# A transformer block on one core: the normalised input transposed by TensorE, or loaded a second time with features on partitions

## The chip, the core and the metric

The kernel runs on one core of a Trainium2 chip. Five engines share the work, each with its own queue of instructions that it executes in order: TensorE (PE) multiplies, VectorE (DVE) and ScalarE (ACT) read its results from PSUM and compute on them, GpSimd (POOL) computes beside them, and the sync engine (SP) issues nearly all DMAs. Engines wait for each other at semaphores. The metric is the device time of one launch in microseconds (us), as the median of several runs.

## The reference

The input x has 4 sequences of 2048 positions with 512 features in float32. The block is a linear-attention layer and a low-rank feed-forward layer, each behind a layer norm and with a residual:

```python
x = x + attn(layernorm(x))            # attn normalises once more: x_norm = layernorm(.) * ln_g + ln_b
# in attn, with z = layernorm(x):
qkv  = x_norm @ W_qkv + b_qkv
gate = sigmoid(z @ W_gate + b_gate); gate = gate / (mean(gate) + EPS)
q, k = relu(q * gate)**2 + EPS, relu(k * gate)**2 + EPS     # 16 heads of 32
kv_s += k_t (x) v_t;  k_s += k_t;  out_t = (q_t . kv_s) / (q_t . k_s + EPS)   # over positions t
return out @ W_proj + b_proj
x = x + gelu(layernorm(x) @ U1 @ V1 + b1) @ U2 @ V2 + b2    # ranks 128, 2048 hidden
```

Two norms in a row come down to a mean and two row factors. With the mean mu and the variance var of a row of x, z = (x - mu) * r with r = (var + EPS)^-1/2, and the second norm multiplies z by (r*r*var + EPS)^-1/2.

## The kernel before

The 64 chunks of 128 positions are taken in turn: step (p, b) starts chunk 4p + b, which is row block p of sequence b. Within a step, one chunk n is projected to gate, key, query and value, the chunk before it (c) goes through scores, state and output projection, the one before that (d) is normalised again and enters the feed-forward layer, which works on groups of two chunks over two steps. So steps differ by the parity of b: an odd step also computes the group's first product with U1 and the last product of an earlier group. Every float32 operand of the large products is split into a high and a low part (float32r tiles named _hi and _lo) and three products are accumulated.

All orders are written out by hand, engine by engine, in the function `step` of each engine. The path of the input that the change touches is:

- SP loads a chunk into `xs`, positions on partitions (`load_x`, L250), three steps ahead.
- DVE takes its mean and variance (`x_stats` L516, `x_moments` L522), at the end of the step two ahead; POOL makes the row factors from them in six operations on one column (`small_stats`, helper L328).
- DVE writes `zs` = (x - mu) * r (`x_norm`, L531), behind the query's evacuation in the step before the chunk's own.
- PE transposes `zs` in four 128x128 blocks into the bank `ps_t` (`tz`, helper `transpose4` L772), behind the output product L964 and ahead of the feed-forward products `h_pair` and `q_pair`. A transpose of the same helper is made of the queries, the keys and the second norm's rows.
- ACT copies the bank to `zt_hi` (`z_head`, L419), DVE subtracts it from the bank into `zt_lo` (`z_tail`, L547). These two are the stationary operands of the four projections (`project`).
- DVE evacuates the gate (L616) and key, query and value (L581, L653), the latter three multiplied by the second row factor.
- POOL adds the output bias to `xs` (`add_bias`, L355), once `zs` is taken, and makes the low parts of the hidden layer and of the keys (`h_tail` L366, L392) around it.

Names in the rows: `ps_q` and `ps_h` are banks of the feed-forward layer, `h_hi` and `h_lo` the parts of its hidden tile, `ot_hi` and `ot_lo` those of the attention output; L979 and L980 are the running sums over the keys, which reuse the bank `ps_b` of that output, and so wait for `ot_lo` (DVE L679). `carry_rows` is a row in DRAM through which the key sums of a sequence go from one row block to the next, stored by L293 and read back to all partitions by L300.

Of the kernel before, what the change touches and what calls it, by code (L numbers as in the profile page):

```python
# [29 lines left out]
P = 128  # L30
# [73 lines left out]
def block_kernel(nc, x, ln_g, ln_b, w_qkv, b_qkv, w_gate, b_gate, w_proj, b_proj,  # L104
                 u1, v1, b1, u2, v2, b2, out, carry_dram):
    ctx = ExitStack()
    with ctx:
# [34 lines left out]
        xs = sb("xs", [P, 4, DM])  # L142
        x1s = sb("x1s", [P, 4, DM])
# [9 lines left out]
        stats, moments = sb("stats", [P, 4, 6]), sb("moments", [P, 4, 2])  # L153
        small = sb("small", [P, 4, 6])
# [22 lines left out]
        def bank(name):  # L177
# [13 lines left out]
            x_stats x_small z_ready xb_ready tz_done zt_hi_ready zt_ready  # L191
# [9 lines left out]
        x_in = [sem(f"x_in{i}") for i in range(4)]  # L201
        stored = [sem(f"stored{i}") for i in range(4)]
# [41 lines left out]
        def _(sp):  # L244
            def load_x(c):
                if not c.exists:
                    return

                wait(sp, s["x1_steps"], Chunk(c.p, c.off - 4).done(3, 1))
                sp.dma_start(xs[:, c.slot, :], x[c.slot, bass.ds(c.row, P), :]).then_inc(x_in[c.slot], 16)  # L250

# [23 lines left out]
            load_tiles(range(8))  # L275
# [5 lines left out]
            def step(p, b):  # L281
                if isinstance(p, int) and 4 * p + b < 2:
                    load_tiles((range(FIRST + 6, FIRST + 9), range(FIRST + 9, len(tiles)))[b])
# [26 lines left out]
        def _(pool):  # L310
# [19 lines left out]
            def small_stats(c):  # L330
# [4 lines left out]
                var, r, done = moments[:, c.slot, 1:2], small[:, c.slot, :], s["x_small"]  # L335
# [4 lines left out]
                pool.wait_ge(done, c.done(6, 1))  # L340
                tiny(r[:, 1:2], r[:, 0:1], minus_half[:, :], ALU.pow, done)
                pool.wait_ge(done, c.done(6, 2))
                tiny(r[:, 2:3], r[:, 1:2], r[:, 1:2], ALU.mult, done)
                pool.wait_ge(done, c.done(6, 3))
                tiny(r[:, 3:4], r[:, 2:3], var, ALU.mult, done)
                pool.wait_ge(done, c.done(6, 4))
                tiny(r[:, 5:6], r[:, 3:4], eps_col[:, :], ALU.add, done)
                pool.wait_ge(done, c.done(6, 5))
                tiny(r[:, 4:5], r[:, 5:6], minus_half[:, :], ALU.pow, done)

            def add_bias(c):

                if c.exists:
                    pool.wait_ge(s["z_ready"], c.done())
# [4 lines left out]
            small_stats(Chunk(0, 0))  # L359
            small_stats(Chunk(0, 1))  # L360
# [8 lines left out]
            def step(p, b):  # L369
# [3 lines left out]
                if d.exists:  # L373
# [3 lines left out]
                        .then_inc(s["x1b_ready"], 1)  # L377
                if ffn.exists and b % 2 == 0 and not is_last(p):
                    h_tail(ffn, pairs[0])
                if n.exists:  # L380
# [3 lines left out]
                        .then_inc(s["key_ready"], 1)  # L384
                if ffn.exists and not is_last(p):
# [3 lines left out]
                add_bias(Chunk(p, b + 1))  # L389
# [19 lines left out]
        def _(act):  # L409
# [6 lines left out]
            def z_head(c):  # L416
                if c.exists:
                    act.wait_ge(s["tz_done"], c.done())
                    E.activation(zt_hi[:, :, :].rearrange(flat), ps_t[:, :], ACT.Copy)\  # L419
                        .then_inc(s["zt_hi_ready"], 1)  # L420
# [9 lines left out]
            tile_heads(range(KT))  # L430
            z_head(Chunk(0, 0))
            tile_heads(range(KT, 6))
# [4 lines left out]
            tile_heads(range(6, FIRST))  # L437
# [67 lines left out]
        def _(dve):  # L505
            E = nc.vector

            def x_stats_wait(c):

                if c.exists:  # L510
                    dve.wait_ge(x_in[c.slot], c.dmas())
                    wait(dve, s["x_small"], Chunk(c.p, c.off - 4).done(6, 6))
# [5 lines left out]
            def x_moments(c):  # L518


                if c.exists:
                    E.bn_aggr(moments[:, c.slot, :], stats[:, c.slot, :]).then_inc(s["x_stats"], 1)  # L522

            def x_norm(c):

                if c.exists:
                    dve.wait_ge(s["x_small"], c.done(6, 2))
                    before = Chunk(c.p, c.off - 3)
                    if before.exists:
# [12 lines left out]
            x_norm(Chunk(0, 0))  # L542
# [21 lines left out]
            tile_tails(range(KT))  # L564
            z_tail(Chunk(0, 0))
            tile_tails(range(KT, 10))
# [34 lines left out]
            def step(p, b):  # L601
# [12 lines left out]
                if n.exists:  # L614
                    dve.wait_ge(s["gate_done"], n.done())
                    E.tensor_tensor(gate[:, :], ps_b[:, :], bias[:, GATE, :], ALU.add)\  # L616
# [8 lines left out]
                    dve.wait_ge(s["x_small"], n.done(6, 6))  # L625
# [18 lines left out]
                x_norm(Chunk(p, b + 1))  # L644
# [92 lines left out]
                if c.exists:  # L737

                    dve.wait_ge(s["x1_small"], c.done(2, 2))
                    after = Chunk(p, b + 1)  # L740
                    if after.exists:
                        dve.wait_ge(s["tz_done"], after.done())
                    elif d.exists:
# [14 lines left out]
        def _(pe):  # L758
# [34 lines left out]
            def tz(c):  # L793
                if not c.exists:
                    return
                pe.wait_ge(s["z_ready"], c.done())
                before = Chunk(c.p, c.off - 2)
                if before.exists:
# [31 lines left out]
            def step(p, b):  # L830
# [16 lines left out]
                if c.exists:  # L847
                    pe.wait_ge(s["den_steps"], c.done(6, 6))

                    if n.exists:  # L850
                        pe.wait_ge(s["zt_ready"], n.done())
# [170 lines left out]
```

## Time and profile before

| | |
|---|---|
| median of 3 runs | 1840.01 us (1838.84 to 1841.26) |
| profiled execution | 1837.18 us |
| its span in the trace | 1835.1 us |
| granted TensorE clock, mean | 0.996 |
| PE busy | 1792.8 us, 98% |
| DVE busy | 1449.0 us, 79% |
| POOL busy | 799.2 us, 44% |
| ACT busy | 683.7 us, 37% |
| DMA | 61.06 MB, 33 GB/s |

The profiled execution is one launch; the span is what the trace covers of it, and some 2 us lie around it. Busy times are unions of the instructions' spans on an engine. A matmul's span in the trace is its latency, and the next one starts before it ends, so what a matmul takes from TensorE is read from the distance of two starts and not from its duration. The profile's lines name tiles as out<-in and the line of the kernel.

### The profile page before, as it was taken

Reading aid. Unit: us, or ns where it says so; the run is one execution under the profiler, and the core shown is the slowest. Engines: PE = TensorE matmul, PEld = TensorE weight load, DVE = VectorE, ACT = ScalarE, POOL = GpSimd, SP = SyncE. Lnnn points to the kernel's source line nnn. Section 1 sums busy time; section 2 is a strip of 40 time slices with the busy share of each in tenths; the row PEclk is TensorE's granted clock in tenths of the full one; section 3 lists DMA queues with packets and bytes.
Section 4 is the critical chain, followed back from the end, with each engine's and each line's share of the span. In section 5 each row is a group of like instructions: output and inputs, shape, how many; then the busy total and the mean of one; then the engine's idle time right before and its main releaser. Section 6 shows DMA issues by size and latency. Waiting matters only on the chain.

```text
span 1835.1 us, 34352 instructions
## 1 busy us (share of the span) xinstructions
PE 1792.8 (98%) x13753; PEld 1535.6 (84%) x13753; DVE 1449.0 (79%) x2606; ACT 683.7 (37%) x1242; POOL 799.2 (44%) x1027
## 2 busy tenths in 40 slices
PE   6899999999999999999999999999999999999997
PEld 3688888888888888888888888888888888888876
DVE  6877888878788788787788788788788788788775
ACT  4233433333433333433333433433333333333332
POOL 3344445434444434444444444444444444354430
PEclk9999999999999999999999999999999999999999
DMA  6101010011010011010010000010100110100000
GB/s 197 39 18 35 24 36 24 24 35 36 24 36 24 24 36 33 26 35 24 24 35 27 33 27 26 31 35 24 36 24 24 36 35 25 35 24 24 29 19 24
DMA packets 34508, 61.06 MB, mean 33 GB/s; under 512 B 3672, under 2 KB 6256, under 8 KB 34352
## 3 DMA queue, kind: packets, MB, share of 16 engines
q1 hardware_dynamic: 33488, 57.31, 9.8%
q8 instruction: 110, 1.80, 0.4%
q10 hardware_dynamic: 864, 1.57, 0.3%
q14 instruction: 46, 0.38, 0.1%
HBM read 41.96 MB, written 16.91 MB: 32 GB/s over the span
## 4 chain that ended last, share of the span: by engine, by line
PE 92%; DVE 1%; POOL 0%; ACT 0%; issue 0%; DVEq 0%
PE ps_a L767 9%; PE ps_a L766 9%; PE ps_a L765 9%; PE ps_t L772 6%; PE ps_b L767 6%; PE ps_b L766 6%; PE ps_b L765 6%; PE ps_q L765 4%; PE ps_b L964 3%; PE ps_h L765 3%; PE ps_h L766 3%; PE ps_h L767 3%; PE ps_q L766 3%; PE ps_q L767 3%; PE ps_c L942 3%; PE ps_c L954 3%
## 5 line engine op out<-in xcount | busy, mean ns | idle before, releaser
L366 POOL TENSOR_TENSOR h_lo<-h_full,h_hi 128x512 fp32r<-128x512 f32 x244 | 313.6, 1285 | 500.0 <-DVE h_hi L593 500.0
L447 ACT ACTIVATE h_full<-ps_h,cols 128x256 f32<-128x256 f32 x512 | 211.0, 472 | 241.6 <-PE ps_h L767 233.8
L593 DVE CAST h_hi<-h_full 128x512 fp32r<-128x512 f32 x256 | 176.1, 688 | 97.4 <-ACT h_full L447 97.4
L765 PE MATMUL ps_b<-wx_hi,zt_hi 128*128 128x512 f32 x512 | 206.0, 402 | 2.0 <-DVE key_sums L695 1.7
L765 PE MATMUL ps_a<-wx_hi,zt_hi 128*128 128x512 f32 x512 | 207.6, 405 | 0.0
L767 PE MATMUL ps_b<-wx_hi,zt_lo 128*128 128x512 f32 x512 | 202.7, 396 | 0.0
L766 PE MATMUL ps_b<-wx_lo,zt_hi 128*128 128x512 f32 x512 | 202.5, 396 | 0.0
L767 PE MATMUL ps_a<-wx_hi,zt_lo 128*128 128x512 f32 x512 | 202.2, 395 | 0.0
L766 PE MATMUL ps_a<-wx_lo,zt_hi 128*128 128x512 f32 x512 | 201.7, 394 | 0.0
L328 POOL TENSOR_TENSOR small<-moments,eps_col 128x1 f32<-128x1 f32 x128 | 25.7, 201 | 394.1 <-DVE moments L734 325.8
L765 PE MATMUL ps_q<-h_hi,u_hi 128*128 128x256 f32 x512 | 159.3, 311 | 7.1 <-DVE h_lo L598 5.1
L458 ACT ACTIVATE query_t<-ps_t 128x512 f32<-128x512 f32 x64 | 38.2, 597 | 323.3 <-PE ps_t L772 323.3
L765 PE MATMUL ps_h<-pt_hi,v_hi 128*128 128x256 f32 x512 | 152.1, 297 | 0.9 <-DVE pt_lo L647 0.9
L766 PE MATMUL ps_h<-pt_lo,v_hi 128*128 128x256 f32 x512 | 144.8, 283 | 0.0
L767 PE MATMUL ps_h<-pt_hi,v_lo 128*128 128x256 f32 x512 | 143.9, 281 | 0.0
L766 PE MATMUL ps_q<-h_lo,u_hi 128*128 128x256 f32 x512 | 143.7, 281 | 0.0
L767 PE MATMUL ps_q<-h_hi,u_lo 128*128 128x256 f32 x512 | 143.5, 280 | 0.0
L765 PEld LDWEIGHTS ps_q<-h_hi,u_hi 128*128 128x128 f32 x512 | 96.4, 188 | 26.1 <-POOL h_lo L366 13.2
L473 ACT ACTIVATE key_t<-ps_t 128x512 f32<-128x512 f32 x64 | 38.3, 598 | 210.7 <-PE ps_t L772 210.7
L767 PEld LDWEIGHTS ps_b<-wx_hi,zt_lo 128*128 128x128 f32 x512 | 96.2, 188 | 23.3
L765 PEld LDWEIGHTS ps_b<-wx_hi,zt_hi 128*128 128x128 f32 x512 | 96.5, 189 | 22.5 <-DVE zt_lo L547 2.1
L767 PEld LDWEIGHTS ps_a<-wx_hi,zt_lo 128*128 128x128 f32 x512 | 96.0, 187 | 22.8
(159 smaller groups left out, 5047.9 us busy)
## 6 DMA issues: line engine op xcount, KB each, us to landing
xs<-L_attn_x SPq DMA_DIRECT2D x64, 256.0 KB, 2.7
out<-x1s SPq DMA_DIRECT2D x64, 256.0 KB, 2.1
key_sums<-carry_rows SPq DMA_DIRECT2D x60, 256.0 KB, 3.2
x1s<-L_attn_W_qkv SPq DMA_DIRECT2D x8, 256.0 KB, 5.1
x1s<-L_attn_W_gate SPq DMA_DIRECT2D x4, 256.0 KB, 4.1
h_full<-L_attn_W_qkv SPq DMA_DIRECT2D x4, 256.0 KB, 6.1
x1s<-L_ffn_U SPq DMA_DIRECT2D x4, 256.0 KB, 3.4
carry_rows<-key_sums SPq DMA_DIRECT2D x64, 2.0 KB
```

What stands on the lines that cost most here:

```text
L366: E.tensor_tensor(h_lo[:, i % 2, :], h_full[:, i % 2, :], h_hi[:, i % 2, :].bitcast(F32), ALU.subtract).then_inc(s["h_lo_ready"], 1)
L447: last = E.activation(h_full[:, i % 2, a * GROUP:(a + 1) * GROUP], ps_h[i % 2][:, a * GROUP:(a + 1) * GROUP], ACT.Gelu_apprx_tanh, bias=b1 ...
L458: E.activation(query_t[:, :, :].rearrange(flat), ps_t[:, :], ACT.Copy)\
L473: E.activation(key_t[:, :, :].rearrange(flat), ps_t[:, :], ACT.Copy)\
L593: E.tensor_copy(h_hi[:, i % 2, :], h_full[:, i % 2, :]).then_inc(s["h_hi_ready"], 1)
L765: E.matmul(ps, wh, mh, start=start and i == 0, stop=False)
L766: E.matmul(ps, wh, ml, start=False, stop=False)
L767: mm = E.matmul(ps, wl, mh, start=False, stop=stop and i == last)
L772: mm = E.transpose(ps_t[:, k * P:(k + 1) * P], src[:, k * P:(k + 1) * P], ident[:, :])
L942: mm = E.matmul(ps_scores[j][:, ft * P:(ft + 1) * P], key_t[rows, ft, :], query_t[rows, ft, :], start=True, stop=True, tile_position=(HEAD ...
L954: mm = E.matmul(ps_c[:, cols], keys[:, c.half, cols], values[:, c.half, cols], start=True, stop=True)
L964: mm = E.matmul(ps_b[HEAD * j:HEAD * (j + 1), ft * P:(ft + 1) * P], values[:, c.half, h * HEAD:(h + 1) * HEAD], probs[:, j, ft * P:(ft + 1 ...
```

## The change

A second copy of the input, laid out with features on partitions (`x_turned`: for each chunk 128 rows of 512 values, four blocks of 128 positions side by side), is passed to the kernel and loaded into `xt`, two chunks deep. The row means go through DRAM to all partitions: SP stores one column of 128 means into `rows_dram` and reads it back as a row of 128 values on every partition (`turn_rows`). POOL subtracts it from `xt` in place (`center`). ACT and DVE make `zt_hi` and `zt_lo` from `xt` in SBUF. `x_norm`, `tz` and the `zs` of the first norm are gone. What stood in `zs` as the factor r now multiplies the gate's evacuation, and the factor of the other three evacuations becomes (var + EPS * (var + EPS))^-1/2, in five operations on a column. `add_bias` follows `center` and stands earlier in POOL's step.

```diff
 def load_x(c):   # SP
     sp.dma_start(xs[:, c.slot, :], x[c.slot, bass.ds(c.row, P), :]).then_inc(x_in[c.slot], 16)
+    wait(sp, s["zt_ready"], Chunk(c.p, c.off - 2).done())
+    sp.dma_start(xt[:, c.half, :, :].rearrange(flat), x_turned[c.slot, c.row // P, :, :])\
+        .then_inc(xt_in[c.slot], 16)
...
+def turn_rows(c):   # SP, at the start of step for Chunk(p, b + 1)
+    sp.wait_ge(s["x_stats"], c.done(2, 2))
+    sp.dma_start(rows_dram[c.slot, :].rearrange("(t a) -> t a", a=1), small[:, c.slot, 2:3]).then_inc(rows_out[c.slot], 16)
+    sp.wait_ge(rows_out[c.slot], c.dmas())
+    wait(sp, s["z_ready"], Chunk(c.p, c.off - 2).done())
+    sp.dma_start(rows[:, c.half, :],
+                 rows_dram[c.slot, :].rearrange("(a t) -> a t", a=1).broadcast_to([P, P]))\
+        .then_inc(rows_in[c.slot], 16)
...
 load_x(Chunk(0, 0))
-load_tiles(range(8))
+load_tiles(range(6))
+turn_rows(Chunk(0, 0))
+load_tiles(range(6, 8))
...
+def center(c):   # POOL
+    mine = xt[:, c.half, :, :]
+    pool.wait_ge(xt_in[c.slot], c.dmas())
+    pool.wait_ge(rows_in[c.slot], c.dmas())
+    E.tensor_tensor(mine, mine, rows[:, c.half, :].unsqueeze(1).broadcast_to([P, KT, P]),
+                    ALU.subtract).then_inc(s["z_ready"], 1)
 def add_bias(c):
-    pool.wait_ge(s["z_ready"], c.done())
+    pool.wait_ge(s["x_stats"], c.done(2, 1))
...
 def z_head(c):   # ACT
-    act.wait_ge(s["tz_done"], c.done())
-    E.activation(zt_hi[:, :, :].rearrange(flat), ps_t[:, :], ACT.Copy)
+    act.wait_ge(s["z_ready"], c.done())
+    act.wait_ge(s["value_done"], before.done())
+    E.activation(zt_hi[:, :, :].rearrange(flat), xt[:, c.half, :, :].rearrange(flat), ACT.Copy)
...
-def x_norm(c):   # DVE
-    dve.wait_ge(s["x_small"], c.done(6, 2))
-    dve.wait_ge(s["tx_done"], before.done())
-    E.tensor_scalar(zs[:, :], xs[:, c.slot, :], moments[:, c.slot, 0:1], small[:, c.slot, 1:2],
-                    ALU.subtract, ALU.mult).then_inc(s["z_ready"], 1)
 def z_tail(c):
-    E.tensor_tensor(zt_lo[:, :, :].rearrange(flat), ps_t[:, :],
+    E.tensor_tensor(zt_lo[:, :, :].rearrange(flat), xt[:, c.half, :, :].rearrange(flat),
                     zt_hi[:, :, :].rearrange(flat).bitcast(F32), ALU.subtract)
...
-    E.tensor_tensor(gate[:, :], ps_b[:, :], bias[:, GATE, :], ALU.add)
+    E.scalar_tensor_tensor(out=gate[:, :], in0=ps_b[:, :], scalar=small[:, n.slot, 1:2],
+                           in1=bias[:, GATE, :], op0=ALU.mult, op1=ALU.add)
...
-def tz(c):   # PE
-    pe.wait_ge(s["z_ready"], c.done())
-    pe.wait_ge(s["probs_ready"], before.done(HPG, HPG))
-    transpose4(zs, s["tz_done"])
-tz(Chunk(0, 0))
...
-    tz(Chunk(p, b + 1))
     if ffn.exists:
         h_pair(ffn, pairs[3])
         q_pair(ffn, pairs[2])
```

On TensorE, in an even step of the steady state, this stands behind the output product L964 before (names as above, zs being the normalised rows):

```order
L964 MATMUL ps_b<-probs,values 32x128 x16
L772 MATMUL ps_t<-ident,zs 128x128 x4
L765 MATMUL ps_h<-pt_hi,v_hi 128x256
L766 MATMUL ps_h<-pt_lo,v_hi 128x256
L767 MATMUL ps_h<-pt_hi,v_lo 128x256
L765 MATMUL ps_h<-pt_hi,v_hi 128x256
L766 MATMUL ps_h<-pt_lo,v_hi 128x256
L767 MATMUL ps_h<-pt_hi,v_lo 128x256
```

And in the changed kernel, where the same product is L980 and the lines of the three-part product are L793 to L795:

```order
L980 MATMUL ps_b<-probs,values 32x128 x16
L793 MATMUL ps_h<-pt_hi,v_hi 128x256
L794 MATMUL ps_h<-pt_lo,v_hi 128x256
L795 MATMUL ps_h<-pt_hi,v_lo 128x256
L793 MATMUL ps_h<-pt_hi,v_hi 128x256
L794 MATMUL ps_h<-pt_lo,v_hi 128x256
L795 MATMUL ps_h<-pt_hi,v_lo 128x256
L793 MATMUL ps_q<-h_hi,u_hi 128x256
```

The four transposes have gone, and the feed-forward products follow the output product at once.

On POOL, an even step before begins with the feed-forward bias (x1s), and has the attention bias (xs) ahead of the keys' low part:

```order
L376 TENSOR_TENSOR x1s<-x1s,bias_out 128x512
L366 TENSOR_TENSOR h_lo<-h_full,h_hi 128x512
L383 TENSOR_TENSOR keys<-keys,eps_col 128x512
L366 TENSOR_TENSOR h_lo<-h_full,h_hi 128x512
L355 TENSOR_TENSOR xs<-xs,bias_proj 128x512
L392 TENSOR_TENSOR key_lo<-keys,key_hi 128x512
L366 TENSOR_TENSOR h_lo<-h_full,h_hi 128x512 x2
```

In the changed kernel L377 is the centering:

```order
L406 TENSOR_TENSOR x1s<-x1s,bias_out 128x512
L377 TENSOR_TENSOR xt<-xt,rows 128x512
L384 TENSOR_TENSOR xs<-xs,bias_proj 128x512
L396 TENSOR_TENSOR h_lo<-h_full,h_hi 128x512
L416 TENSOR_TENSOR keys<-keys,eps_col 128x512
L396 TENSOR_TENSOR h_lo<-h_full,h_hi 128x512
L427 TENSOR_TENSOR key_lo<-keys,key_hi 128x512
L396 TENSOR_TENSOR h_lo<-h_full,h_hi 128x512 x2
```

The centering and the attention bias now stand between the feed-forward bias and the first low part of the hidden tile.

On SP, the end of an even step and the start of an odd one before, from the second load on (key_sums is the read of the carried sums, out the store of results):

```order
L250 DMA xs<-L_attn_x 128x512
L254 DMA out<-x1s 128x512 x2
L293 DMA carry_rows<-key_sums 1x512
L300 DMA key_sums<-carry_rows 128x512
L250 DMA xs<-L_attn_x 128x512
```

And in the changed kernel, from the load of xs on (L264 and L267 are the two DMAs of `turn_rows`):

```order
L254 DMA xs<-L_attn_x 128x512
L256 DMA xt<-x_turned 128x512
L264 DMA turned_rows<-small 128x1
L267 DMA rows<-turned_rows 128x128
L273 DMA out<-x1s 128x512 x2
L315 DMA carry_rows<-key_sums 1x512
L322 DMA key_sums<-carry_rows 128x512
L254 DMA xs<-L_attn_x 128x512
```

The load of `xt` and the two DMAs of the means now stand ahead of the stores and of the carried sums.

## Rows read from the trace of the kernel before

**Rows 1.** The page: busy time and share of each engine; the chain by engine.
```profile
PE 1792.8 (98%) x13753; PEld 1535.6 (84%) x13753; DVE 1449.0 (79%) x2606; ACT 683.7 (37%) x1242; POOL 799.2 (44%) x1027
...
PE 92%; DVE 1%; POOL 0%; ACT 0%; issue 0%; DVEq 0%
```

**Rows 2.** Two neighbouring steps: stretch, then busy us and instructions of each engine.
```profile
868.00:897.22 29.22, 29.19 (x227) 25.16 (x225) 23.22 (x43) 10.78 (x20) 12.67 (x16) 1.00 0.12 37
897.22:923.33 26.11, 26.11 (x208) 22.60 (x207) 21.20 (x39) 10.22 (x18) 12.51 (x16) 1.00 0.08 22
```

**Rows 3.** TensorE, odd step: start us, us, engine, line, operation, out<-in, shape, count.
```profile
891.09 0.66 PE L772 MATMUL ps_t<-ident,zs 128*128 128x128 f32 x4
891.50 0.36 PE L765 MATMUL ps_h<-pt_hi,v_hi 128*128 128x256 f32 x1
...
892.07 0.28 PE L766 MATMUL ps_h<-pt_lo,v_hi 128*128 128x256 f32 x1
892.18 0.28 PE L767 MATMUL ps_h<-pt_hi,v_lo 128*128 128x256 f32 x1
892.43 0.39 PE L765 MATMUL ps_q<-h_hi,u_hi 128*128 128x256 f32 x1
...
893.25 0.39 PE L979 MATMUL ps_b<-key_hi,causal 128*128 128x512 f32 x1
```

**Rows 4.** TensorE, even step, the same columns.
```profile
913.21 0.38 PE L765 MATMUL ps_q<-h_hi,u_hi 128*128 128x256 f32 x1
...
917.43 0.66 PE L772 MATMUL ps_t<-ident,zs 128*128 128x128 f32 x4
917.85 0.36 PE L765 MATMUL ps_h<-pt_hi,v_hi 128*128 128x256 f32 x1
...
919.36 0.39 PE L979 MATMUL ps_b<-key_hi,causal 128*128 128x512 f32 x1
```

**Rows 5.** Weight-load waits over 125 to 1740 us: waiter, releaser, us, times, longest.
```profile
PEld ps_q L765 <- POOL h_lo L366: 11.7, 59, 0.3
```

**Rows 6.** GpSimd, odd step at 888, even step from 910; idle before in brackets.
```profile
888.43 1.28 POOL L355 TENSOR_TENSOR xs<-xs,bias_proj 128x512 f32<-128x512 f32 x1
...
891.10 1.28 POOL L366 TENSOR_TENSOR h_lo<-h_full,h_hi 128x512 fp32r<-128x512 f32 x1
...
910.39 1.29 POOL L366 TENSOR_TENSOR h_lo<-h_full,h_hi 128x512 fp32r<-128x512 f32 x1 [5.35 <-DVE h_hi L593]
...
915.53 1.30 POOL L392 TENSOR_TENSOR key_lo<-keys,key_hi 128x512 fp32r<-128x512 f32 x1
```

**Rows 7.** VectorE, odd step at 891, even step from 901.
```profile
891.86 0.69 DVE L679 TENSOR_TENSOR ot_lo<-ps_b,ot_hi 128x512 fp32r<-128x512 f32 x1 [0.77 <-ACT ot_hi L491]
...
901.26 0.17 DVE L522 BATCH_NORM_AGGREGATE moments<-stats 128x2 f32<-128x6 f32 x1
...
915.80 1.30 DVE L593 CAST h_hi<-h_full 128x512 fp32r<-128x512 f32 x1
...
918.24 0.69 DVE L679 TENSOR_TENSOR ot_lo<-ps_b,ot_hi 128x512 fp32r<-128x512 f32 x1
```

**Rows 8.** VectorE groups by line and form: count, busy us, mean ns, idle before.
```profile
L584 DVE SCALAR_TENSOR_TENSOR keys<-keys,gate_scale,gate 128x512 f32<-128x512 f32 x64 | 73.6, 1150 | 2.3
L584 DVE SCALAR_TENSOR_TENSOR queries<-queries,gate_scale,gate 128x512 f32<-128x512 f32 x64 | 48.8, 762 | 2.3
```

**Rows 9.** The sync engine's DMA issues late in an odd step.
```profile
895.75 0.24 SPq L293 DMA_DIRECT2D carry_rows<-key_sums  x1
896.91 0.33 SPq L300 DMA_DIRECT2D key_sums<-carry_rows  x1
```

**Rows 10.** DMA issues: tensors, queue, count, KB each, us to landing.
```profile
key_sums<-carry_rows SPq DMA_DIRECT2D x60, 256.0 KB, 3.2
x1s<-L_attn_W_qkv SPq DMA_DIRECT2D x8, 256.0 KB, 5.1
```

**Rows 11.** TensorE in the second step of the run, before the feed-forward work starts.
```profile
65.74 0.51 PE L979 MATMUL ps_b<-key_hi,causal 128*128 128x512 f32 x1 [0.87 <-DVE ot_lo L679]
```

More of the change, by code:

```diff
@@ L142, in block_kernel @@
         xs = sb("xs", [P, 4, DM])
+        xt = sb("xt", [P, 2, KT, P])
+        rows = sb("rows", [P, 2, P])
         x1s = sb("x1s", [P, 4, DM])
@@ L201, in block_kernel @@
         x_in = [sem(f"x_in{i}") for i in range(4)]
+        xt_in = [sem(f"xt_in{i}") for i in range(4)]
+        rows_out = [sem(f"rows_out{i}") for i in range(4)]
+        rows_in = [sem(f"rows_in{i}") for i in range(4)]
         stored = [sem(f"stored{i}") for i in range(4)]
@@ L359, in _ @@
             small_stats(Chunk(0, 0))
+            center(Chunk(0, 0))
             small_stats(Chunk(0, 1))
@@ L417, in z_head @@
                 if c.exists:
-                    act.wait_ge(s["tz_done"], c.done())
-                    E.activation(zt_hi[:, :, :].rearrange(flat), ps_t[:, :], ACT.Copy)\
+                    act.wait_ge(s["z_ready"], c.done())
+                    before = Chunk(c.p, c.off - 1)
+                    if before.exists:
+                        act.wait_ge(s["value_done"], before.done())
+                    E.activation(zt_hi[:, :, :].rearrange(flat), xt[:, c.half, :, :].rearrange(flat), ACT.Copy)\
                         .then_inc(s["zt_hi_ready"], 1)
@@ L428, in tile_heads @@
                     E.activation(hi, stage(t), ACT.Copy, scale=scale).then_inc(s["stage_hi"], 1)
-            tile_heads(range(KT))
-            z_head(Chunk(0, 0))
-            tile_heads(range(KT, 6))
+            tile_heads(range(6))
             b_row = b_qkv.rearrange("(a n) -> a n", a=1)
@@ L436, in _ @@
                     .then_inc(s["biases"], 16)
-            tile_heads(range(6, FIRST))
+            tile_heads(range(6, 8))
+            z_head(Chunk(0, 0))
+            tile_heads(range(8, FIRST))
             act.dma_start(bias_proj[:, :], b_proj.rearrange("(a n) -> a n", a=1).broadcast_to([P, DM]))\
@@ L511, in x_stats_wait @@
                     dve.wait_ge(x_in[c.slot], c.dmas())
-                    wait(dve, s["x_small"], Chunk(c.p, c.off - 4).done(6, 6))
+                    before = Chunk(c.p, c.off - 4)
+                    wait(dve, s["x_small"], before.done(5, 5))
+                    if before.exists:
+                        dve.wait_ge(rows_out[c.slot], before.dmas())
             def x_stats(c):
@@ L562, in tile_tails @@
                             .then_inc(s["stage_lo"], 1)
-            tile_tails(range(KT))
+            tile_tails(range(8))
             z_tail(Chunk(0, 0))
-            tile_tails(range(KT, 10))
+            tile_tails(range(8, 10))
             first_stats(1)
@@ L615, in step @@
                     dve.wait_ge(s["gate_done"], n.done())
-                    E.tensor_tensor(gate[:, :], ps_b[:, :], bias[:, GATE, :], ALU.add)\
+                    dve.wait_ge(s["x_small"], n.done(5, 2))
+                    E.scalar_tensor_tensor(out=gate[:, :], in0=ps_b[:, :], scalar=small[:, n.slot, 1:2],
+                                           in1=bias[:, GATE, :], op0=ALU.mult, op1=ALU.add)\
                         .then_inc(s["gate_evac"], 1)
@@ L739, in step @@
                     dve.wait_ge(s["x1_small"], c.done(2, 2))
[L740 to L743, printed above, removed]
+                    if d.exists:
                         dve.wait_ge(s["tx_done"], d.done())
@@ L977, in step @@
                         pe.wait_ge(s["ot_ready"], c.done())
+                    else:
+                        pe.wait_ge(s["query_steps"], n.done(3, 1))
                     pe.wait_ge(s["key_lo_ready"], n.done())
```

59 lines of the change are left out of this document (29 added, 30 removed).

## The prediction, made before the changed kernel was run

> **What bounds the kernel now.** I read the page's busy times first, then its chain, then two neighbouring steps by window, then the stretch around the removed transposes on each engine. TensorE is busy 1792.8 of 1835.1 us and carries 92% of the chain that ends last [rows 1]. The reader should see in the windows that this is no average over unlike stages: an odd step takes 29.22 us with 29.19 on TensorE, an even one 26.11 with 26.11, while VectorE has 23.22 and 21.20 and GpSimd 12.67 and 12.51 [rows 2]. So in the steady state TensorE never waits, and what it no longer issues is time saved, as long as nothing that the removed work covered comes late. The rest of the reading is therefore about cover.
>
> **What is removed on TensorE.** Four transposes per chunk. Their cost is the distance of starts, since the spans overlap: in the odd step they start at 891.09 and the next product at 891.50, which is 0.41 us [rows 3]; in the even step 917.43 to 917.85, 0.42 us [rows 4]. The product behind them starts with a longer first distance either way, since the output product ahead of it is in float32 like the transposes, so I leave that out of the gain.
>
> In the odd step there is a second, smaller piece. Products of this size follow each other at 0.11 us (892.07, 892.18), but the next one, which reads the hidden tile's low part, comes at 892.43, 0.25 later, so some 0.13 us is a wait [rows 3]. The view of waits puts such waits of the weight loads down to POOL's low part, 59 of them, 11.7 us together, so it is the rule and no accident [rows 5]. POOL makes that low part at 891.10, done at 892.38, behind the attention bias (888.43, 1.28 us) and the keys' low part [rows 6]. The attention bias moves out of this place to the start of the step's POOL work, so the low part is due about 1 us earlier, at 891.4; TensorE then asks for it at 892.30 - 0.41 = 891.89. The wait goes: 0.13 more in an odd step, 0.54 together.
>
> **Which chunks count.** The transposes for chunk 0 stand in the start. For chunks 1 to 3 there is no feed-forward work behind them, and TensorE waits for the attention output's low part at L979 anyway, 0.87 us in the second step [rows 11]: removing 0.4 us only lengthens that wait. Chunks 4 to 63 are 60, half in odd steps: 30 x 0.54 + 30 x 0.42 = 28.8 us.
>
> **What is late next.** L979 reuses the bank of the attention output and needs VectorE's low part of it. Odd step: that ends at 891.86 + 0.69 = 892.55 [rows 7], and TensorE would now ask at 893.25 - 0.54 = 892.71 [rows 3]. Covered, by 0.16. Even step: it ends at 918.24 + 0.69 = 918.93 [rows 7], and TensorE asks at 919.36 - 0.42 = 918.94 [rows 4]. That is a tie; with a few hundredths for the semaphore the even step could lose 0.05. Against it, the cast of the hidden tile at 915.80, which stands ahead of it on VectorE, takes 1.30 us beside the keys' low part on POOL at 915.53 [rows 6, 7]; that low part too moves forward by the 1.28 of the attention bias, and the cast should shorten. I charge 0.02 x 30 = 0.6 us, with 0 and 3 as ends (none; 0.1 each time). Sum 28.2.
>
> **Edits that I cost at nothing in the steady state.** On VectorE the pass of the first norm goes, the gate's evacuation gains a multiplication, and `z_tail` reads two SBUF tiles instead of one and a PSUM bank. No row here shows the last in its place; the nearest is one operation with SBUF inputs alone, 762 ns where it is undisturbed and 1150 ns where it runs beside POOL [rows 8], so its price is between 0 and 0.39 us, and I take 0, since POOL's neighbouring work lies before and after it. The cover is VectorE's idle time, 6.0 us in an odd step and 4.9 in an even one [rows 2]; without it, up to 0.39 a step. `z_head` on ACT reads SBUF instead of PSUM, in its old place. POOL gains the centering, for which I take the 1.28 of the bias pass, the same shape [rows 6]; it has 16.6 us of idle time in an odd step and 13.6 in an even one [rows 2].
>
> The centering waits for the means to go through DRAM, and what is queued behind it on POOL is, in an even step, the attention bias and the first low part of the hidden tile, for which TensorE waits at 913.21 [rows 4]. The means are there at 901.26 + 0.17 = 901.43 [rows 7]. The store and its landing: a stored row of 2 KB lets the next DMA go 1.16 us after its own issue (895.75, 896.91) [rows 9]; a read to all partitions lands after 3.2 us for 256 KB, four times what is read here [rows 10]. So POOL can go at 901.43 + 1.16 + 3.2 = 905.8, and with the store as slow as that read at 907.8. It must go by 913.21 - 1.29 - 2 x 1.28 = 909.4. Slack 1.6 to 3.6 us, so nothing. In the odd step the keys' addition stands ahead of the centering, and there is more room. SP, which waits for the store's landing, has the result stores and the carried sums queued behind it; both wait for work that comes much later in the step, the carried sums until 895.75 in the step from 868 [rows 2, 9].
>
> **The start.** Two loads of 256 KB more and the round trip of the means stand ahead of the weight tiles on SP's queue before the first projection. Weight loads land after 5.1 us there [rows 10]. Ends: 0, if the additional loads run beside what waits anyway, and 6.3, one such landing plus one store of 1.16. I take 2, nearer to the store, since the tiles that are held up are few.
>
> **Sum.** -28.2 + 2 = -26.2 us. On the profiled execution's 1837.18 (span 1835.1) that is 1811; it ran 2.8 us under the median of the runs shown, 1840.01, on which the sum gives 1813.8. I forecast 1814 us.
>
> **Rivals.**
>
> Start dearer (A): the steady state as above, but the start costs the upper end. 1814 + 4 = 1818 us. For it: SP's queue is in order and the round trip stands in its middle. Against: chunk 0 needs all its weights anyway.
>
> VectorE and POOL collide in the stretch before L979 (B): there is no slack there in the even step, and POOL's work is rearranged around it. At the 0.39 us of [rows 8] once a step, less 0.1 of slack, 60 x 0.29 = 17 us are lost: 1831 us. Against it, POOL's moves take work out of that stretch and none into it. The Trainium skill (SBUF — State Buffer, Who interferes with whom) has the harsher rule: a VectorE instruction with two SBUF inputs and a GpSimd instruction that reads SBUF exclude each other for the whole instruction. The trace agrees that they disturb each other, but shows 0.39 us in the mean. A full exclusion in this place as a mechanism of its own (B2), at the 1.28 of a POOL pass [rows 6], would lose 60 x 1.18 = 71 us: 1885.
>
> The means come late (C), the other side: POOL stands at the centering of each even step, the low part of the hidden tile comes late, TensorE waits at the first product that reads it. It costs from a round trip of 909.4 - 901.43 = 8.0 us on, 30 us for each us beyond; from 8.0 + 28.2 / 30 = 8.9 us on the kernel is slower than before. A round trip of 9.5 us gives 1814 + 45 = 1859 us. For it: 128 single values are stored, of 4 bytes each, and no row shows such a store. The Trainium skill (DMA: Bandwidth & Descriptors, Specifications) says that transfers under 512 bytes are done by read-modify-write; no run here shows it. Against: [rows 9, 10] give 4.4 us, and twice the slower landing is 6.4.
>
> **How the numbers follow.** Forecast 0.74, with a range of its own of 1809 to 1821; A 0.10; B 0.10, of which 0.03 ends within 0.2% of before (3.7 us, about what a measurement of this kernel can tell from no change); B2 0.02; C 0.04. Faster by over 0.2%: 0.74 + 0.10 + 0.07 = 0.91; within: 0.03; slower: 0.06. The range reaches down by a start that costs nothing, with some hidden gain, to 1808, and up into B, to 1828.
>
> **What would show it.** Right: the starts of the output product and of the feed-forward product behind it follow directly, both steps are shorter by 0.4 to 0.5 us, with TensorE still busy in all of them; the wait for POOL's low part is about halved in the weight loads; the first gate product starts some 2 us later. Wrong: a wait at L979 for the attention output (B), POOL idle at the centering past 909 in the even step's terms with TensorE waiting for the hidden tile's low part (C), or steps shorter by the 0.4 us but a start that is later by more than 6 us.

## The result, and the profile after

The changed kernel takes 2149.23 us (median of 4 runs, 2139.50 to 2152.98), the kernel before 1840.32 (1838.84 to 1841.26): a ratio of 1.1674, 95% interval 1.1647 to 1.1702. The forecast was 1814 us. The profiled execution took 2139.5 us. Its page, in the form of [rows 1], and the mean granted clock of its core:

```profile
PE 1858.6 (87%) x13497; PEld 1601.0 (75%) x13497; DVE 1378.6 (64%) x2542; ACT 675.1 (32%) x1242; POOL 859.4 (40%) x1027
...
PE 3%; DVE 1%; DMA 1%; ACT 0%; POOL 0%; issue 0%; DVEq 0%; POOLq 0%
```

```profile
core 0: 2137.8 us, clock 0.942
```

The page counts 256 instructions fewer on TensorE, the transposes that the change removes. TensorE is nevertheless busy for longer, in a span that it no longer fills. The chain is followed back only a few per cent here, so its shares are no guide; the waits are. The columns are waiter, releaser, us in all, times, longest; first the engines, then the sync engine (SP).

```profile
POOL xt L377 <- DMA rows<-turned_rows: 522.5, 64, 11.7
...
PEld ps_q L793 <- POOL h_lo L396: 235.7, 61, 5.5
...
PE ps_q L793 <- POOL h_lo L396: 224.1, 60, 5.3
```

```profile
SPq L267 <- DMA turned_rows<-small: 478.2, 64, 9.3
```

In [rows 5] the weight loads wait for POOL's low part 0.2 us each time; now they do so for 3.9 us in the mean. POOL stands at the centering (L377) and waits for the turned means, and SP waits 7.5 us for each store of them (L267). One round trip, first SP's issues, then VectorE's moments, then POOL, up to the low part that TensorE needs, and the product on TensorE that waited for it:

```profile
1054.24 0.33 SPq L264 DMA_DIRECT2D turned_rows<-small  x1
1061.81 0.33 SPq L267 DMA_DIRECT2D rows<-turned_rows  x1
```

```profile
1054.04 0.17 DVE L563 BATCH_NORM_AGGREGATE small<-stats 128x2 f32<-128x6 f32 x1
```

```profile
1067.00 1.27 POOL L377 TENSOR_TENSOR xt<-xt,rows 128x512 f32<-128x512 f32 x1 [9.57 <-DMA rows<-turned_rows]
1068.22 1.26 POOL L384 TENSOR_TENSOR xs<-xs,bias_proj 128x512 f32<-128x512 f32 x1
1069.44 1.26 POOL L396 TENSOR_TENSOR h_lo<-h_full,h_hi 128x512 fp32r<-128x512 f32 x1
```

```profile
1070.76 0.58 PE L793 MATMUL ps_q<-h_hi,u_hi 128*128 128x256 f32 x1 [4.97 <-POOL h_lo L396]
```

Moments done at 1054.21, store issued at once, read issued 7.57 us later, centering 5.2 us after that: 12.8 us in all, called the trip below. The view of DMAs has the medians (KB each, us to landing), and one row of the kernel before for the result store:

```profile
out<-x1s SPq DMA_DIRECT2D x64, 256.0 KB, 5.1
...
rows<-turned_rows SPq DMA_DIRECT2D x64, 64.0 KB, 4.8
...
turned_rows<-small SPq DMA_DIRECT2D x64, 0.5 KB, 7.7
```

```profile
out<-x1s SPq DMA_DIRECT2D x64, 256.0 KB, 2.1
```

On TensorE an even step and an odd one; in brackets the idle time before:

```profile
1006.29 0.58 PE L793 MATMUL ps_q<-h_hi,u_hi 128*128 128x256 f32 x1 [5.30 <-POOL h_lo L396]
1006.67 0.41 PE L794 MATMUL ps_q<-h_lo,u_hi 128*128 128x256 f32 x1
1006.89 0.41 PE L795 MATMUL ps_q<-h_hi,u_lo 128*128 128x256 f32 x1
...
1039.91 0.39 PE L793 MATMUL ps_q<-h_hi,u_hi 128*128 128x256 f32 x1 [2.45 <-POOL h_lo L396]
1040.14 0.28 PE L794 MATMUL ps_q<-h_lo,u_hi 128*128 128x256 f32 x1
1040.26 0.28 PE L795 MATMUL ps_q<-h_hi,u_lo 128*128 128x256 f32 x1
```

Both kinds of step wait. Behind the long wait the products also follow each other at 0.22 us instead of 0.12: the clock. The windows behind that wait and a little later, then one behind a wait of 2.45 us two steps on, and then the two steps as in [rows 2] (the last three figures are granted clock, DMA share, GB/s):

```profile
1006.29:1011.50 5.21, 5.21 (x24) 5.21 (x25) 0.95 (x3) 1.47 (x3) 4.28 (x4) 0.50 0.01 3
1012.00:1018.00 6.00, 6.00 (x61) 5.12 (x61) 4.34 (x7) 1.85 (x4) 1.30 (x1) 1.00 0.00 0
```

```profile
1104.55:1110.40 5.85, 5.85 (x27) 5.63 (x27) 1.67 (x6) 0.84 (x2) 3.69 (x3) 0.50 0.00 0
```

```profile
986.90:1018.40 31.50, 26.20 (x194) 22.92 (x193) 17.72 (x35) 10.09 (x18) 13.39 (x16) 0.89 0.07 22
1018.40:1051.30 32.90, 30.45 (x230) 26.28 (x230) 23.86 (x45) 10.63 (x20) 13.68 (x16) 1.00 0.14 46
```

TensorE ran at half clock (1.2 instead of 2.4 GHz) for the 5.2 us after the 5.30 us wait, and at full clock after the 2.45 us one at 1039.91. The same wait of 2.45 us before 1104.55 was followed by half clock again. From 200 to 2000 us the clock was at half behind all 28 waits of the even steps (4.9 us in the mean), and for at least a part of the next 3 us behind 15 of the 27 of the odd steps (2.5 us in the mean).

### The profile page after: what moved, and what is told of

The parts are those of the page before. It is cut to its first block and busy times, and to the rows that moved or that the text cites. A ratio compares the mean times of both kernels' runs of the same rounds, so it can differ in the third digit from the quotient of the medians.

```text
span 2137.8 us, 34097 instructions
## 1 busy us (share of the span) xinstructions
PE 1858.6 (87%) x13497; PEld 1601.0 (75%) x13497; DVE 1378.6 (64%) x2542; ACT 675.1 (32%) x1242; POOL 859.4 (40%) x1027
## 5 line engine op out<-in xcount | busy, mean ns | idle before, releaser
L793 PE MATMUL ps_q<-h_hi,u_hi 128*128 128x256 f32 x512 | 176.2, 344 | 229.2 <-POOL h_lo L396 224.1
L623 DVE CAST h_hi<-h_full 128x512 fp32r<-128x512 f32 x256 | 135.8, 532 | 364.3 <-ACT h_full L485 364.3
L793 PEld LDWEIGHTS ps_q<-h_hi,u_hi 128*128 128x128 f32 x512 | 112.6, 220 | 245.0 <-POOL h_lo L396 235.7
L377 POOL TENSOR_TENSOR xt<-xt,rows 128x512 f32<-128x512 f32 x64 | 83.9, 1311 | 522.5 <-DMA rows<-turned_rows 522.5
L793 PE MATMUL ps_a<-wx_hi,zt_hi 128*128 128x512 f32 x512 | 207.6, 405 | 0.0
L793 PE MATMUL ps_b<-wx_hi,zt_hi 128*128 128x512 f32 x512 | 206.2, 403 | 0.9 <-DVE key_sums L726 0.9
L795 PE MATMUL ps_b<-wx_hi,zt_lo 128*128 128x512 f32 x512 | 202.9, 396 | 0.0
L795 PE MATMUL ps_a<-wx_hi,zt_lo 128*128 128x512 f32 x512 | 202.2, 395 | 0.0
L793 PE MATMUL ps_h<-pt_hi,v_hi 128*128 128x256 f32 x512 | 163.9, 320 | 0.9 <-DVE pt_lo L678 0.9
L794 PE MATMUL ps_q<-h_lo,u_hi 128*128 128x256 f32 x512 | 159.5, 312 | 0.0
L795 PE MATMUL ps_q<-h_hi,u_lo 128*128 128x256 f32 x512 | 158.2, 309 | 0.0
L795 PE MATMUL ps_h<-pt_hi,v_lo 128*128 128x256 f32 x512 | 154.8, 302 | 0.0
L350 POOL TENSOR_TENSOR small<-moments,eps_col 128x1 f32<-128x1 f32 x64 | 12.2, 190 | 318.7 <-DVE moments L765 318.7
L793 PEld LDWEIGHTS ps_h<-pt_hi,v_hi 128*128 128x128 f32 x512 | 107.2, 209 | 16.3 <-issue 12.3
L794 PEld LDWEIGHTS ps_q<-h_lo,u_hi 128*128 128x128 f32 x512 | 113.6, 222 | 2.8
L795 PEld LDWEIGHTS ps_b<-wx_hi,zt_lo 128*128 128x128 f32 x512 | 96.5, 189 | 23.4
```

The costliest lines, as they stand in the source:

```text
L350: E.tensor_tensor(out_, a, b, op).then_inc(sem_, 1)
L377: E.tensor_tensor(mine, mine, rows[:, c.half, :].unsqueeze(1).broadcast_to([P, KT, P]), ALU.subtract).then_inc(s["z_ready"], 1)
L623: E.tensor_copy(h_hi[:, i % 2, :], h_full[:, i % 2, :]).then_inc(s["h_hi_ready"], 1)
L793: E.matmul(ps, wh, mh, start=start and i == 0, stop=False)
L794: E.matmul(ps, wh, ml, start=False, stop=False)
L795: mm = E.matmul(ps, wl, mh, start=False, stop=stop and i == last)
```

## Experiments

Two theories stood at first. **H**: POOL's in-order queue stands at the centering, and the round trip alone is the loss. **L**: the trip is long because the store is 128 writes of 4 bytes into one 512-byte row of DRAM, which land one after another. The rivals of L: small descriptors are slow wherever they go (S), the number of descriptors counts, or the store waits behind the loads of the input ahead of it on its queue (Q). Each experiment is the changed kernel with one edit, beside new runs of the kernel before (medians 1838.3 to 1839.7). Store lines are shown without the semaphore at their end, and only the lines that ask the question: where the centering reads something else than the means, the expectation names it. "From store to read" is the time between the issues of the two DMAs, as a median.

**One row from one partition.**

```diff
-  sp.dma_start(rows_dram[c.slot, :].rearrange("(t a) -> t a", a=1), small[:, c.slot, 2:3])
+  sp.wait_ge(s["consts_pool"], 7)
+  sp.dma_start(rows_dram[c.slot:c.slot + 1, :], ident[0:1, :])
```

> The store of the means is one row of 512 bytes from one partition (a row of the identity instead of the means, so the centering subtracts something else). Theory L (128 writes of 4 bytes into the same 512 bytes of DRAM land one after another) and theory S (a write of 4 bytes is slow wherever it goes): the store lets SP go on after about 1.2 us as the row of the carried sums does, the read lands in 3 us or less, POOL centers 4 to 5 us after the moments, and the steady state is what was predicted: 1812 to 1825 us. Theory Q (the store waits behind the 256 KB load of xt that SP issued just before): the store still takes some 7 us, the time stays near 2149.

1817.43 us (1816.0 to 1818.2), ratio 0.9890 (0.9873 to 0.9906). From store to read 1.09 us. The store stands in the same place of the queue, so Q falls.

**The same 128 values, 512 bytes apart.**

```diff
+  sp.dma_start(rows_dram[c.slot, :, 0:1], small[:, c.slot, 2:3])     # rows_dram (4, 128, 128)
```

> The same 128 values of 4 bytes are stored, but 512 bytes apart in DRAM; the read takes 128 values of another tensor (of ln_b), so the centering subtracts something else. Theory L: the writes no longer meet, the store lands in 2 to 3 us, the time is 1812 to 1830. Theory S: the store lands in 7 to 8 us as before and the time stays at 2100 to 2150. Theory Q: as S.

1821.04 us (1816.92 to 1821.35), ratio 0.9903 (0.9888 to 0.9918). Still 128 writes of 4 bytes:

```profile
turned_rows<-small SPq DMA_DIRECT2D x64, 0.5 KB, 1.4
```

The store lands in 1.4 us, not 7.7. S falls, and so does the number of descriptors.

**128 rows of 512 bytes.**

```diff
+  sp.wait_ge(s["consts_pool"], 7)
+  sp.dma_start(rows_dram[c.slot, :, :], ident[:, :])                 # rows_dram (4, 128, 128)
```

> 128 descriptors again, but of 512 bytes each, to 128 rows of DRAM (the identity is stored, its first row read back, so the centering subtracts something else). Theories L and S: the store lands in 2 to 3 us, the time is 1812 to 1830. A theory that it is the number of descriptors, whatever their size: 7 us and 2100 to 2150.

1819.71 us (1818.65 to 1820.55), ratio 0.9901 (0.9886 to 0.9915); 128 times the bytes land in 1.5 us.

**The centering later on POOL**, behind the next piece of the feed-forward, with its DMAs as they are:

```diff
-                if b % 2 == 0:
-                    center(Chunk(p, b + 1))
-                    add_bias(Chunk(p, b + 1))
+                add_bias(Chunk(p, b + 1))
...
-                if b % 2:
-                    center(Chunk(p, b + 1))
-                    add_bias(Chunk(p, b + 1))
...
+                center(Chunk(p, b + 1))
```

> The changed kernel with all its DMAs, the centering moved behind the second low part of the hidden tile in POOL's step, the attention bias ahead of it; nothing is left out. Theory H (the loss is POOL standing at the centering with the low parts of the hidden tile behind it): the store still lands after 7.7 us, but TensorE no longer waits; the third low part stays where it was before the change, so the odd step gains nothing and the even one some 0.1 us, and the start is 4.6 us later: 1836 to 1848 us. If DMA traffic, the input read from SBUF on ACT and VectorE or the colder TensorE were the cause in themselves: above 1950.

1860.13 us (1858.83 to 1861.49), ratio 1.0121 (1.0106 to 1.0136). The store is as slow as ever and most of the loss is gone, which is what H says (DMAs, then waits):

```profile
out<-x1s SPq DMA_DIRECT2D x64, 256.0 KB, 5.0
...
rows<-turned_rows SPq DMA_DIRECT2D x64, 64.0 KB, 4.5
...
turned_rows<-small SPq DMA_DIRECT2D x64, 0.5 KB, 7.0
```

```profile
PE ps_q L789 <- POOL h_lo L396: 11.9, 32, 0.9
...
PE ps_t L796 <- DVE x1t_lo L637: 9.6, 33, 1.4
```

The time is 12 us above the expectation. These two waits come to 21.5 us; why the new order brings the second was not followed.

**No DMA: TensorE spreads the means** by one more product for each chunk, and ScalarE copies it to `rows`. In the odd step the centering also moves ahead of the keys' addition on POOL, to where it stands in the even step:

```diff
+  E.matmul(ps[:, 0:P], small[:, c.slot, 2:3].broadcast_to([P, P]), ident[:, :], start=True, stop=True)
...
+  E.activation(rows[:, c.half, :], ps[:, 0:P], ACT.Copy)
```

> Nothing of the computation is left out. The means go by no transfer at all: TensorE multiplies the mean's column, spread over 128 columns, by the identity, one product for each chunk right behind the second norm's transposes, and ScalarE copies the 128x128 result to SBUF for GpSimd's pass. Theory L (the 128 four-byte writes into one 512-byte row land one after another, and the wait for them is the whole loss): the loss is gone. The pair of steps is that of the run with a one-row store (54.56 us) and two products more, about 0.1 us each: some 54.8 us a pair, and over 30 pairs 1820 us, within 1816 to 1826. If centering on GpSimd itself were what costs (its pass of 1.3 us before h_lo), this kernel would stay above 1840, since it keeps that pass where it is. No four-byte store is left, so the result stores should land in about 2.1 us again instead of 5.1.

1833.13 us (1831.66 to 1834.31), ratio 0.9961 (0.9948 to 0.9975): above the range, though under 1840, so GpSimd's pass itself is not what costs. A pair of steps takes 55.01 us instead of the 54.56 of the expectation, so a product costs 0.22 us and not 0.1: the line of it shows two instructions for each, and that is most of the error of the expectation.

```profile
1014.20 0.39 PE L813 MATMUL ps_d<-ident,small 128*128 128x128 f32 x2
```

**VectorE turns the means first**, in 32x32 blocks, so that the store is 4 writes of 128 bytes:

```diff
+  E.transpose(turned[:, c.slot, :], moments[:, c.slot, :]).then_inc(s["x_turn"], 1)
...
+  sp.dma_start(rows_dram[c.slot, :].rearrange("(i t) -> i t", t=32), turned[0:P:32, c.slot, :])
```

> Nothing of the computation is left out. VectorE transposes the moments in 32x32 blocks at the end of its step, so that the 128 means stand in 4 partitions, and the store is 4 descriptors of 128 bytes into the same 512-byte row, instead of 128 of 4 bytes. The read that spreads the row is that of the changed kernel, as soon as the store has landed. Theory L: a chain of 4 writes is short, so that the store lands in 1.2 to 1.6 us (7.7 with 128 writes), and the read in about 2.8 to 3.2 us; the centering is never late and the time is 1817 to 1822 us. If instead the read is slow because it reads a row that was just written (the runs with short stores either read another row or one written in whole rows), the read stays near 4.8 us, the round trip is some 6.5 us, and the time still falls under 1830 us, since the slack is 8.0 us.

**1819.34 us (1817.09 to 1821.76), ratio 0.9889 (0.9875 to 0.9902): nothing of the computation is left out, and it is faster than both kernels.** First SP's issues, then VectorE, then the page (span and busy times), the wait for POOL's low part, and a window of two steps:

```profile
1003.97 0.51 SPq L265 DMA_DIRECT2D turned_rows<-turned  x1
1005.53 0.33 SPq L268 DMA_DIRECT2D rows<-turned_rows  x1
```

```profile
1003.73 0.21 DVE L569 STREAM_TRANSPOSE turned<-moments 128x32 f32<-128x32 f32 x1
```

```profile
span 1817.6 us, 34163 instructions
...
PE 1768.5 (97%) x13497; PEld 1513.4 (83%) x13497; DVE 1461.4 (80%) x2607; ACT 675.6 (37%) x1242; POOL 895.0 (49%) x1027
```

```profile
PEld ps_q L803 <- POOL h_lo L397: 8.1, 31, 1.1
```

```profile
1000.00:1054.55 54.55, 54.51 (x424) 47.03 (x423) 44.74 (x81) 20.73 (x38) 28.13 (x32) 1.00 0.13 42
```

The store is over in 1.56 us, the read in 2.8, though it reads the row that was just written.

**Sixteen means side by side, the eight groups 512 bytes apart.**

```diff
+  sp.dma_start(rows_dram[c.slot, :, 0:16].rearrange("g (t a) -> g t a", a=1), small[:, c.slot, 2:3])
```

> As the run with the means 512 bytes apart, but with 16 means side by side in 64 bytes and the eight groups 512 bytes apart; the centering reads a row of the constants instead of the means, so its output is not the reference's. It asks how large the piece of memory is in which writes wait for each other. If it is the 512-byte row (Theory L as stated): the chains are 16 long instead of 128, and by 7.7 us for 128 and 1.4 us for 1 in a row the store lands in about 2.2 us, the time is some 1820 us. If it is a piece of 64 bytes, the chain was 16 long before too: the store stays near 7.7 us and the time near 2149 us. If neither, but the number of descriptors with a neighbour, something between.

1820.57 us (1818.48 to 1821.86), ratio 0.9894 (0.9881 to 0.9908). From store to read 2.1 us, as a chain of 16 would give; a piece of 64 bytes alone is not it.

**Two rows, four rows.** The means 8 and 16 bytes apart.

```diff
+  sp.dma_start(rows_dram[c.slot, :, 0:1], small[:, c.slot, 2:3])     # rows_dram (4, 128, 2) or (4, 128, 4)
```

> The 128 four-byte means go 8 bytes apart, 64 into each of two 512-byte rows; the centering reads a row of the constants instead of the means, so its output is not the reference's. From store to the next issue it took 1.41 us with one write in a row, 2.05 with 16 and 7.75 with 128: 0.043 to 0.050 us for each further write. Theory L, linear in the writes of a row: 64 writes take 4.1 to 4.6 us. With a read of about 3 us the round trip is some 7.5 us, inside the slack of 8.0 us that the prediction named, so 1818 to 1830 us. If what costs were a fixed effect of neighbours in memory and not a chain, the store would stay at 7 to 8 us and the time near 2149 us.

> The same with means 16 bytes apart, 32 into each of four 512-byte rows; the centering reads a row of the constants, so its output is not the reference's. Theory L: 1.41 us and 31 further writes of 0.043 to 0.050 us, 2.7 to 3.0 us from store to read; the round trip is some 6 us, the time 1817 to 1822 us.

1824.77 us (1823.12 to 1824.93) and 1821.01 us (1819.83 to 1822.24). The stores, first of two rows, then of four:

```profile
turned_rows<-small SPq DMA_DIRECT2D x64, 0.5 KB, 3.0
```

```profile
turned_rows<-small SPq DMA_DIRECT2D x64, 0.5 KB, 1.4
```

From store to read it takes 2.97 and 1.41 us, both less than expected (4.1 to 4.6, 2.7 to 3.0). So L holds in its core (dense four-byte writes are slow, spread ones not), and its line does not: beyond the 1.4 us of a write in each row, 32 writes in a row 16 bytes apart cost nothing, 64 cost 1.6 us, 128 cost 6.3, and 16 side by side cost 0.7. Neither a piece of 512 bytes nor one of 64 explains all four. In what piece of memory they wait for each other stays open.

**Nobody waits for the slow store.** The read takes a row of constants and follows at once:

```diff
-  sp.wait_ge(rows_out[c.slot], c.dmas())
...
-  rows_dram[c.slot, :].rearrange("(a t) -> a t", a=1).broadcast_to([P, P])
+  ln_b[0:P].rearrange("(a t) -> a t", a=1).broadcast_to([P, P])
```

> The changed kernel's store of 128 four-byte writes into one row is kept, but nothing waits for it except the reuse of the moments four chunks later: the centering reads a row of the constants instead of the means, at once, so its output is not the reference's. Theory H (the loss is the wait for the round trip, at GpSimd's in-order queue): the store still takes about 7 us, and the time is that of the runs with a quick store, 1817 to 1822 us. If the slow store itself disturbs the other transfers (result stores landing in 5.1 us instead of 2.1, loads of the input behind them) and that is part of the loss, the time stays above 1825 us, and above 1840 if it is the larger part.

1833.67 us (1832.84 to 1835.93), ratio 0.9969 (0.9959 to 0.9980): the second case, above 1825 and under 1840, but by a transfer that the expectation did not name. The read, now right behind the store on the same queue, is held up by it; the same read behind the spread store landed in 2.8 us:

```profile
rows<-L_attn_ln_b SPq DMA_DIRECT2D x64, 64.0 KB, 6.9
...
turned_rows<-small SPq DMA_DIRECT2D x64, 0.5 KB, 7.1
```

So the centering still comes late, at 7.4 us after the moments, and the store disturbs what is queued behind it. The result stores land after 4.2 us here, issued over 5 us behind the read, and after 3.2 us in the run with three reads below, where no store is slow and they too are issued 0.4 us behind a read: the 5.1 us of the changed kernel has some of both.

**A long trip without a slow store.** The kernel with the block transpose, and the row read two or three times over, each read waiting for the one before:

```diff
+  sp.dma_start(rows[:, c.half, :], rows_dram[c.slot, :]...).then_inc(rows_mid0[c.slot], 16)
+  sp.wait_ge(rows_mid0[c.slot], c.dmas())
```

> Nothing of the computation is left out. The kernel with the block transpose on VectorE (store 1.56 us, read 2.8 us, 1819 us), and the row is read twice, the second read issued when the first has landed, so that the round trip is some 7.4 us with no slow store in it. If the slack is 8.0 us as predicted, this costs nothing or little: 1818 to 1826 us. If the slack is shorter, by some 60 waits a run and us: at a slack of 6 us about 1880 to 1900 us.

> Nothing of the computation is left out. The same with three reads in a row: the round trip is some 10.4 us. It asks for the price of each us past the slack without a slow store. By the prediction's rival (only every other step waits, 30 us for each us past 8.0): 1819 + 2.4 x 30 = about 1890 us. By the changed kernel's own loss (330 us at a round trip of 12.8 us, both steps waiting and TensorE's clock at half for a while behind each long wait, 69 us for each us): 1819 + 2.4 x 69 = about 1985 us. Near 1820 would mean that the length of the round trip was never the cause, and the slow store alone was.

1837.94 us (1835.47 to 1840.28) and 1968.73 us (1961.18 to 1972.19), ratios 1.0001 (0.9991 to 1.0010) and 1.0708 (1.0679 to 1.0736). Two reads come 12 us above their range; three lie between the price of rival C (1890) and that of the changed kernel (1985), nearer to the latter. With three reads the waits and the half clock of the changed kernel are back, with no slow store in it (waits, then the clock):

```profile
PEld ps_q L813 <- POOL h_lo L407: 119.7, 61, 3.6
PE ps_q L813 <- POOL h_lo L407: 108.0, 60, 3.4
```

```profile
core 0: 1966.3 us, clock 0.973
```

The runs on one line, by the trip from the end of the moments to the start of the centering (medians of the odd and of the even steps between 200 and 1700 us, read from VectorE and POOL):

| trip, odd / even, us | time, us | kernel |
|---|---|---|
| 6.0 / 4.4 | 1821.0 | 512 bytes apart |
| 6.1 / 4.8 | 1819.3 | block transpose |
| 6.1 / 6.0 | 1824.8 | two rows |
| 7.5 / 7.4 | 1833.7 | nobody waits |
| 7.9 / 7.7 | 1837.9 | read twice |
| 10.7 / 10.5 | 1968.7 | read three times |
| 12.8 / 12.7 | 2149.2 | as changed |

The other four with a quick store (one row, 512-byte rows, sixteen side by side, four rows) lie at 6.0 to 6.1 / 4.1 to 5.2 and 1817 to 1821 us; in the odd steps the keys' addition stands right ahead of the centering and keeps them at 6. Whatever makes the trip long, the time follows it: nearly flat to 6, some 19 us dearer by 7.8, then 47 us for each us to 10.6 and 84 for each us beyond. And with the centering moved back on POOL it starts 16.3 / 13.5 us after the moments, later than in any row here, at 1860 us: what costs is the work behind it in POOL's queue. H is shown.

## Why the prediction was wrong

**The step that failed** is the centering's round trip, costed at 1.16 + 3.2 = 4.4 us with 6.4 as its upper end, and so at nothing. It took 12.8. The store's 1.16 came from a row of 2 KB stored from one partition [rows 9]; 128 single values into 512 bytes took 7.6. I had named that no row showed such a store, and still took the upper end of the trip from rows of other shapes. The read's 3.2 [rows 10] took 5.2 to the centering; with a quick store it lands in 2.8. Why it is slower behind the slow one stays open.

On the rule that the prediction cited from the Trainium skill (DMA: Bandwidth & Descriptors, Specifications), read-modify-write under 512 bytes: size alone is not what costs here, since the same four-byte writes spread out land in 1.4 us. That such writes hold each other up when they lie close would fit it; no run shows the mechanism.

**Rival C was the right mechanism, with a chance of 0.04 and too low a price.** Its slack of 8.0 us was good: a wait of 4.97 us at a trip of 12.8 puts it at 7.8, and so do all 28 waits of the even steps (7.82 in the mean); the runs at 7.4 and 7.8 are the first to lose much. Its 30 us for each us counted the even steps alone. By its rule the mean trip of 12.7 us would cost 30 x 4.7 = 141 us, 1955. On top come 30 x 0.2 = 6 for the slack, 30 x 2.5 = 75 for the odd steps, which "more room" did not cover, and the clock: the same 13,497 instructions kept TensorE busy 1858.6 us at a granted 0.942, instead of 1768.5 with the quick store at 0.994, 90 us more. 1955 + 6 + 75 + 90 = 2126, against 2139.5 of the execution that these rows are from and a median of 2149; the rest was not followed.

**The removed transposes: right.** 0.41 + 0.42 = 0.83 us a pair were predicted. With the block transpose their 0.41 us are gone from either step (means over 25 steps of each kind, as in the next two points), and the next product follows at once.

**The wait for POOL's low part in the odd step: obtained, and more than was named.** 0.13 us a pair were to go; 0.23 went, since the product at 892.43 and the one behind it were both late [rows 3] and now follow at 0.12. The waits of the weight loads fall from 59 [rows 5] to 29 in the same stretch.

**What is late next: a tie that was priced too low.** For the bank of the attention output the prediction charged 0.02 us in an even step and nothing in an odd one. TensorE waits there in both: the weight load comes 0.05 us after VectorE's low part is done, and the next product follows 0.33 us behind the first instead of 0.23. That is 0.10 in an even and 0.11 in an odd step, 6 us in the run instead of 0.6. Before, and then with the block transpose, an odd step:

```profile
892.65 0.28 PE L766 MATMUL ps_q<-h_lo,u_hi 128*128 128x256 f32 x1
...
893.48 0.39 PE L980 MATMUL ps_b<-key_lo,causal 128*128 128x512 f32 x1
```

```profile
994.30 0.28 PE L805 MATMUL ps_h<-pt_hi,v_lo 128*128 128x256 f32 x1
...
994.38 0.69 DVE L719 TENSOR_TENSOR ot_lo<-ps_b,ot_hi 128x512 fp32r<-128x512 f32 x1 [0.78 <-ACT ot_hi L530]
994.42 0.28 PE L803 MATMUL ps_q<-h_hi,u_hi 128*128 128x256 f32 x1
...
994.54 0.28 PE L804 MATMUL ps_q<-h_lo,u_hi 128*128 128x256 f32 x1
...
995.12 0.19 PEld L1006 LDWEIGHTS ps_b<-key_hi,causal 128*128 128x128 f32 x1
995.13 0.50 PE L1006 MATMUL ps_b<-key_hi,causal 128*128 128x512 f32 x1
...
995.46 0.39 PE L1007 MATMUL ps_b<-key_lo,causal 128*128 128x512 f32 x1
```

A pair of steps took 55.36 us before and 54.57 with the block transpose (means over 29 pairs), 0.80 less instead of the 0.94 predicted: 0.82 + 0.23 - 0.21, less 0.04 because the product behind the output product takes 0.22 us to the next where behind a transpose it took 0.20. The odd step gained 0.49 and the even one 0.30; 0.4 to 0.5 in both was the sign of being right. Rivals B and B2 expected longer work on VectorE at this place; its low part takes 0.69 us as before [rows 7], so they have no place in these runs.

**The edits at nothing: right.** TensorE fills 54.51 of 54.55 us with the block transpose.

**The start: too low.** 2 us were taken, 6.3 was the upper end. The first gate product came at 23.03 us before and at 27.64 as changed, 4.6 later; with quick stores at 23.3 to 25.9. In the fifth step the block transpose is 4.25 us behind the kernel before (132.77 against 128.52), about halfway between the 2 and rival A's 6.3.

**The sum, with the trip mended:** in 59 steps from there 23.5 us are gained, the start is 4.25 dearer and the end 1.7 longer: 1835.1 - 23.5 + 4.25 + 1.7 = 1817.6, the span measured. By the prediction's terms it would have been 1835.1 - 28.2 + 2 = 1808.9. So its 1814 is 5 us under the 1819 of the kernel with a short trip, and inside its range of 1809 to 1821: these smaller errors together would not have left it.

## What to carry to other kernels

A trip through DRAM that another engine's in-order queue waits for is to be priced by the shape of its writes, not by its bytes; where no row shows that shape, its upper end is open, and the slack has to be compared with that and not with the nearest landing. Turn a column into a few long pieces on the chip before it is stored (0.21 us on VectorE here), or place its values apart; no run here reads a row back that was stored apart, so what that read costs is open. When a wait falls on the bounding engine, count every kind of step that has it, and the slower clock behind it.

## What the runs showed of the hardware

- 128 writes of 4 bytes took 7.7 us to land in DRAM side by side, 3.0 at 8 bytes apart, 1.4 at 16 bytes and at 512. 128 rows of 512 bytes took 1.5.
- A 64 KB read issued 0.4 us behind such a store on the same queue landed after 6.9 us, instead of 2.8.
- TensorE's granted clock was 0.50 for the 5.2 us behind a wait of 5.30 us, and as low behind some waits of 2.45 us while 1.00 behind others; over the run the slower products took 90 us more, beside 224 us of the waits themselves.
- A float32 product of 128x128 by 128x128 is two instructions here and cost 0.22 us in a full queue.
